# A fused attention and expert kernel on one core: VectorE's statistics, slots and residual moved within the group step, the rank matmuls one tile earlier

## The reference

```
h0  = layernorm(x)
g   = sigmoid(h0 @ Wg.T + bg)
h   = associative_scan of h[l] = (1 - g[l]) * h[l-1] + g[l] * h0[l], along the 1024 tokens
x1  = x + layernorm(h @ Wo.T + bo)
xf  = layernorm(x1)
eid = argmax(softmax(xf @ router_w + router_b))        # one of 8 experts
rank = running number of the token within its expert
y   = relu(xf @ w1[eid] + b1[eid]) @ w2[eid] + b2[eid] if rank < 320
      else relu(xf @ ow1 + ob1) @ ow2 + ob2             # overflow network, hidden size 1024
out = x1 + layernorm(y)
```

## Time and profile before

| | |
|---|---|
| median of 3 runs | 1272.75 us (1271.8 to 1273.87) |
| the profiled execution, its own time | 1271.02 us |
| its span, first to last instruction | 1269.3 us |
| granted TensorE clock, mean | 0.98 |
| PE busy | 1172.6 us, 92% of the span |
| DVE, POOL, ACT busy | 1003.3, 810.3 and 772.5 us |
| one step of the main loop, from one projection to the next | 552.84 to 586.09 us, 33.25 us |

### The profile page before, as it was taken

How to read it: one execution, slowest core, us unless ns; L and a number is a source line. 1 busy time by engine, 2 the same in 40 slices (tenths; PEclk the granted TensorE clock), 3 DMA queues, 4 the chain that set the end, 5 groups by cost and what they waited for, 6 DMA issues and landing times. The chain is left out here.

```text
span 1269.3 us, 24820 instructions
## 1 busy us (share of the span) xinstructions
PE 1172.6 (92%) x7705; PEld 1038.1 (82%) x7705; DVE 1003.3 (79%) x2731; ACT 772.5 (61%) x1362; POOL 810.3 (64%) x887
## 2 busy tenths in 40 slices
PE   4499999999999999999999999999999999889994
PEld 4388888888888888888888888888888888789994
DVE  4688888888888888888888888888888876578882
ACT  4265666666666666666666666666665655477773
POOL 4456666666666666666666666666666664436774
PEclk9699999999999999999999999999999999999997
DMA  7211111111111110100111110011111100334430
GB/s 242 83 35 50 51 47 44 38 37 34 33 33 33 33 33 33 33 26 24 33 33 33 33 33 25 25 33 33 33 33 33 33 17 18 104 112 168 149 103 31
DMA packets 59688, 65.32 MB, mean 51 GB/s; under 512 B 7836, under 2 KB 55886, under 8 KB 59525
## 3 DMA queue, kind: packets, MB, share of 16 engines
q1 hardware_dynamic: 52484, 59.58, 14.5%
q0 software_dynamic: 7168, 5.32, 1.4%
HBM read 40.17 MB, written 38.87 MB: 62 GB/s over the span
## 5 line engine op out<-in xcount | busy, mean ns | idle before, releaser
L362 POOL TENSOR_TENSOR rstd<-veps,mhalf 128x4 f32<-128x4 f32 (+1 forms) x144 | 179.4, 1246 | 355.1 <-DVE nmean L712 355.1
L539 ACT ACTIVATE hid<-psH,biasT 128x512 f32<-128x512 f32 (+1 forms) x320 | 209.1, 653 | 264.4 <-PE psH L1010 259.2
L1108 PE MATMUL psY<-W_hi,hid_hi 128*128 128x256 f32 x1216 | 351.2, 289 | 0.9 <-DVE hid_lo L833 0.9
L1111 PE MATMUL psY<-W_hi,hid_lo 128*128 128x256 f32 x1216 | 344.2, 283 | 0.0
L1110 PE MATMUL psY<-W_lo,hid_hi 128*128 128x256 f32 x1216 | 344.0, 283 | 0.0
L833 DVE TENSOR_TENSOR hid_lo<-hid,hid_hi 128x512 fp32r<-128x512 f32 (+1 forms) x320 | 266.0, 835 | 89.3 <-ACT hid_hi L543 83.8
L1008 PE MATMUL psH<-xfT_hi,W_hi 128*128 128x512 f32 (+1 forms) x640 | 246.1, 385 | 5.5 <-DVE xfT_lo L777 2.9
L1010 PE MATMUL psH<-xfT_hi,W_lo 128*128 128x512 f32 (+1 forms) x640 | 242.5, 379 | 0.0
L1009 PE MATMUL psH<-xfT_lo,W_hi 128*128 128x512 f32 (+1 forms) x640 | 242.3, 379 | 0.0
L1108 PEld LDWEIGHTS psY<-W_hi,hid_hi 128*128 128x128 f32 x1216 | 230.2, 189 | 10.5 <-DVE hid_lo L833 1.8
L1110 PEld LDWEIGHTS psY<-W_lo,hid_hi 128*128 128x128 f32 x1216 | 230.0, 189 | 6.7
(11 more groups left out here) (110 smaller groups left out, 2186.6 us busy)
## 6 DMA issues: line engine op xcount, KB each, us to landing
xin<-L_attn_x SPq DMA_DIRECT2D x32, 512.0 KB, 3.5
stage<-L_ffn_w SPq DMA_DIRECT2D x16, 1024.0 KB, 6.2
out<-outt SPq DMA_DIRECT2D x32, 512.0 KB, 2.9
xbuf<-zrow SPq DMA_DIRECT2D x1, 2570.0 KB, 18.5
xin<-xbuf SPq DMA_DIRECT2D x8, 257.0 KB, 5.5
stage<-L_ffn_ow SPq DMA_DIRECT2D x2, 1024.0 KB, 10.3
xbuf<-x,idx POOLq DMA_INDIRECT x128
b_b<-L_ffn_b SPq DMA_DIRECT2D x1, 1024.0 KB, 13.5
```

What stands on the lines that cost most here:

```text
L362: pool.tensor_tensor(rstd[k][:, 0:n], veps[k][:, 0:n], mhalf[:, 0:n], ALU.pow).then_inc(s_rs[k], 1)
L539: act.activation(hid[j % 2][:, 0:n], psH[:, j % 2, 0:n], ACT.Relu, bias=bias).then_inc(s_hid, 1)
L1108: pe.matmul(psY_t[:, t, :], hi, w[0][:, j, :], start=(j == 0 and t % 2 == 0), stop=False, skip_group_check=True)
L1111: last = pe.matmul(psY_t[:, t, :], lo_, w[0][:, j, :], start=False, stop=(j == HC - 1), skip_group_check=True)
```

## The change

Three queues are written in another order; no instruction is added or removed.

- **DVE.** `stats1(nxt)` comes directly behind `attended(nxt)`, ahead of `lo(2)`. `place(now)` comes behind `lo(2)`. Behind `lo(3)` stand `residual1(nxt)` and the four `bn_stats` of `stats2`, then `xn_lo(far)`, then the `moments` of `stats2`, and then `lo(4)` and `lo(5)`.
- **ACT.** `norm1(nxt)` comes ahead of `xn_hi(far)` and of tile 4's two activations, where it stood behind both.
- **PE.** `rank(now)` comes behind layer 1's tile 3 (the fourth), ahead of layer 2's tile 1, where it stood behind tile 4.

```diff
--- before.py
+++ after.py
@@ -618,11 +618,11 @@
                 if live(grp(i, u, -1), NG):
                     norm3(grp(i, u, -1), TG)
                 hidden(range(2, 4))
+                if up:
+                    norm1(nxt)
                 if ahead:
                     xn_hi(far)
                 hidden(range(4, 5))
-                if up:
-                    norm1(nxt)
                 if not ahead:
                     for j in range(4 * u, 4 * u + 4):
                         weights_hi((0, 0), j)
@@ -767,9 +767,13 @@
                 dve.wait_ge(s_u, cnt(g, 1, 1))
                 dve.tensor_tensor(x1[v][:, :, 0:D], att[:], xin[v][:], ALU.add).then_inc(s_x1, 1)
 
+            def read_rows2a(g):
+                dve.wait_ge(s_x1, cnt(g, 1, 1))
+                read_rows(2, lambda t: x1[g[1]][:, t, 0:D], TG)
+
             def stats2(g):
-                dve.wait_ge(s_x1, cnt(g, 1, 1))
-                stats(2, lambda t: x1[g[1]][:, t, 0:D], g, TG)
+                read_rows2a(g)
+                moments(2, g, TG)
 
             def xf_lo(g, n, base=0):
                 for c in range(DC):
@@ -879,19 +883,19 @@
                     choose(now)
                 if up:
                     attended(nxt)
+                    stats1(nxt)
                 low(2)
+                if run:
+                    place(now)
+                low(3)
                 if up:
-                    stats1(nxt)
-                low(3)
+                    residual1(nxt)
+                    read_rows2a(nxt)
                 if ahead:
                     xn_lo(far)
-                if run:
-                    place(now)
-                low(4)
                 if up:
-                    residual1(nxt)
-                    stats2(nxt)
-                low(5)
+                    moments(2, nxt, TG)
+                low(4, 5)
                 if ahead:
                     recurrence(far)
                 else:
@@ -1129,7 +1133,7 @@
                         layer1(now, j, GT, W1[1])
                         if j == 2 and live(grp(i, u, -1), NG):
                             pe.wait_ge(s_y, cnt(now, 2, 0))
-                        if j == 4:
+                        if j == 3:
                             rank(now)
                         layer2(now, j - 2, TG, W2[1])
                     if j == 3 and ahead:
```

## The result

| | before | after |
|---|---|---|
| median of the measurement | 1272.28 us (1271.61 to 1273.87, 4 runs) | 1282.64 us (1281.23 to 1284.62, 4 runs) |
| ratio, 95% interval | | 1.0081 (1.0063 to 1.0098) |
| span of the profiled execution | 1269.3 us | 1279.5 us |
| PE, DVE, ACT, POOL busy | 1172.6, 1003.3, 772.5, 810.3 us | 1169.3, 995.7, 766.5, 840.5 us |
| from one projection to the next, mean of 30 | 32.98 us | 33.48 us |

The change made the kernel slower by 10 us, and the forecast of 1255.5 us (1247 to 1268) was wrong. But this is not the kernel's only time: in the last group of experiments the same text took 1240.1 us against 1270.4, a ratio of 0.976.

A forecast was written before the change was run, and what follows sets the result against it. PE's queue, busy 92% of the span, was taken as the bound. Savings of 30 x 0.49 + 2.0 + 0.6 = 17.3 us from 1271.02 gave 1253.7, and 1.7 for the median gave 1255.5 us, range 1247 to 1268.

The forecast's parts named there:

- the chain: From `att`'s early statistics through POOL, `norm1`, residual and `tok2` to PE's transposes, forecast to start 0.49 us earlier each step.
- the gate's wait of 0.67 in all 30 steps: PE's `gate(far)` would wait for `xn_lo`, now behind the residual's reads, starting at 568.79 instead of 568.12.
- first rival: The gate hardly waits, POOL's `rstd` taking 1.0 instead of 1.4 or gate inputs coming closer: 1246.5 us, chance 0.10.
- Behind the loop: Last group's transposes gain 2.0 us of a 2.88 us wait, first expert's transposes 0.6 of 4.46.
- POOL is in `residual2` until 558.26 + 2.39 = 560.65: POOL's `rstd` for the early statistics could start only at 560.65, when `residual2` ends, instead of 559.61.
- third rival: `xn_lo`'s chain from POOL's `outt` makes the gate's wait outgrow the removed one: slower, 1276 us, chance 0.10.
- its point of 0.58 us on: Delay of the gate's chain, 0.49 + 2.6 / 30 = 0.58 us, from which the slower rival decides.
- Ranks and slots at nothing: Earlier rank matmuls on PE and `place` on DVE were both costed at nothing.
- the right cover: `place` takes the statistics' position ahead of `lo(3)`; were it gone, `lo(3)`, the residual and the gate would be late.
- these statistics run at their old length: On DVE, `att`'s statistics were taken to run beside POOL's `outt` at their old length.
- the sum: For `tok2`: two writes ahead of DVE's second scan, two behind `lo(6)`, ending at 576.94 instead of 577.68.
- the second rival: `tok2` is held off: three POOL writes stay behind `lo(6)`, each step saves 0.3 us: 1261 us, chance 0.18.

The follow-up runs named there:

- dispatch_first: Changed kernel with POOL's scatter DMAs (`dispatch`) ahead of norm 2 in its queue: 1238.74 us, and 1239.51 us in a second run.
- runs with one DMA: One scatter DMA per group instead of four, the other tiles' rows left out: 1242.94 us in the changed kernel, 1267.06 us in the kernel before.
- memset kernels: Changed kernel with memsets on POOL ahead of the scatter DMAs: three (0.8 us) took 1258.18 us, one (0.2 us) 1239.64 and 1240.23 us.
- norm 0 first: Changed kernel with norm 0 ahead of the third deviation on POOL: 1234.83 us with `dispatch_first`, 1300.21 us with the DMAs in the change's place.
- fourth group: Reruns on one chip: changed kernel unaltered 1283.02 us, kernel before 1270.77, `dispatch_first` 1239.51, norm 0 first without `dispatch_first` 1300.21.

## Why the prediction was wrong

**Where no release is late (1240.1 us), the chain was right in every other step.** Behind the projection I had `outt` until 7.81, the second `rstd` at 16.53, the gate at 15.95 with a new wait of 0.67, `tok2` from 18.51 to 24.10, the transposes at 24.40 without a wait. The step at 603.84 has 7.90, 16.57, 15.95 with 0.66, 18.50 to 24.14, and 24.46. The trade of one wait for the other is as described. That the gate agrees to 0.01 us is in part luck: I let `rstd` start directly behind `outt`, and it starts 0.18 us behind (it waits for `veps` and `nmean`, see the last section); against that, `nmr` took 0.20 us and not 0.30, and `norm1` follows it by 0.04 us, as it did in the earlier trace rows, where my sum has 0.12.

**The term that was mis-sized there is the gate's wait of 0.67 in all 30 steps.** In 13 it is nothing: `outt` starts 4.8 us behind the projection (576.94 - 572.16) instead of 5.5, and `rstd` and `nmr` of `deviation(3)` ahead of it take 1.04 and 0.20 us instead of 1.42 and 0.65, since no low half of DVE starts just ahead of either of them. My first rival had a `rstd` of 1.0 instead of 1.4, but the one in its sum is that of `deviation(1)`, which takes 1.39 us in both kinds of step; it had the result near (1246.5) and the place wrong. 13 x 0.66 is 8.6 us. The mean distance between projections fell by 32.98 - 32.06 = 0.92 us; of that the two waits explain 0.76 and 0.16 was not followed (5 us in all). Behind the loop 3.5 us are gained: the last `transposes1` waits 0.6 us instead of 3.0 (forecast 2.0), and the first expert's transposes 3.3 instead of 4.5 (forecast 0.6). The first projection comes 0.9 us later than in the kernel before, which the forecast doesn't have and no run explains. Together 30.2 us, the difference of the two spans; the medians differ by 30.3.

**Where releases are late (1282.64 us), the step that failed is "POOL is in `residual2` until 558.26 + 2.39 = 560.65".** It took over `outt`'s place from the kernel before, 5.42 us behind the projection, with its end at 7.81. It was 6.59, with the end at 8.99, by the late `ysb`. The gate's pause of 1.8 us instead of 0.67 outweighs the 1.16 removed: the mean distance is 33.48, 1.42 above the undisturbed 32.06, and 30 x 1.42 = 42.6 us is the difference between the two times (42.5). That is my third rival, "the gate's wait outgrows the one removed", from its point of 0.58 us on, with the place (POOL's `outt`) right and a cause that it didn't name. I gave it 0.10. The trace of before did show the late release, 0.04 and 0.65 us in turn at `ysb`; I never looked at that eviction, since PE's wait in the kernel before didn't hang on it.

**Ranks and slots at nothing is right in the sum, and says the wrong thing of what they do.** I named the right cover and the wrong reason for the gate to wait: with this part left undone the rest of the change costs about 51 us more (1291.4 against 1240.1, on two chips), since `psA` isn't free for the gate. No run shows what this part is worth where releases are late.

**The change needs these of its parts.** With no late releases: ScalarE's order and `xn_lo` undone 1286, rank and slots undone 1291, `xn_lo` ahead of the residual 1260 (with `dispatch_first`), all 1240. The place of `att`'s statistics was not undone by itself. The late releases fall on the whole change and hardly on the kernel before, whose wait at `tok2` hides 0.65 us.

**Still open** is what makes the increments late. What the runs show: where it occurred, it needed the scatter DMAs near layer 2's end (69 late with the changed kernel, 0 with the DMAs first, on the same occasion), and it needs something that differs between occasions with the same program. The runs with one DMA don't bear on this: on their occasion no run had a late increment, with four DMAs either. Whether that is the chip, its neighbours or where the program was loaded was not tried. All runs with late increments also lack more than half of the scatter DMAs' records, though `dispatch_first` lacks 812 with none late; and every timed run here was a recorded one (each has its span and clock), so the recording may itself have a part in it. The Trainium skill, page "NOTIFIC — the notification-queue block", section "7.1 Overflow: three behaviours, one of which stalls the engine", says that a full queue of records drops new ones, overwrites the oldest or stalls the producer, as it is set. The first two would fit the missing records and the third the late increments; one queue does not do both, and no run here shows any of them. The memset kernels and the one with ScalarE's old order were never run on an occasion with late releases.

The version to keep is `dispatch_first`: 1238.74 and 1239.51 us, one on either kind of occasion, against 1240 or 1283 for the change alone. With norm 0 first it took 1234.83 us, on one occasion.

## What to carry to other kernels

A change that removes a wait takes the slack from chains nobody looked at: before you forecast, follow the new critical chain back past the first engine that only "keeps its place", and look for waits there that are longer than the work they wait for. Run the unaltered kernel beside its variants before you credit an edit with a gain; four experiments agreed here with a theory that the plain kernel, on a further chip, corrected. And a buffer that serves three tenants (`psA`) makes the reader of the second one a waiter of the third.

## What was not expected of the hardware

- **A semaphore of PE can rise up to 1.8 us behind its matmul** while indirect DMAs of POOL are in flight (1.79 us in the step shown); on another occasion, with the DMAs at the same distance (4.04 us from the first issue to layer 2's end), not at all. In the page it looks like idle time with the releaser "remote" (60.3 us).
- **A small DVE instruction waits for a large one of POOL.** `veps`, 128 x 4 elements, took 1.41 us under `outt` and 0.17 us without it (DVE's rows above), and it ended 0.02 us behind `outt` (599.77 + 1.41, 598.76 + 2.40). The Trainium skill, page "SBUF — State Buffer", section "Who interferes with whom", says that `tensor_scalar` can enter a mode that takes the port pair shared with GpSimd, and that whoever is second is fully blocked. The trace agrees: in the first run of the changed kernel `veps` was held in 29 of 29 cases under `outt`, with a median of 1.9 us, and the median of the other 115 is 0.17 us. My prediction had told only half of that section (two SBUF inputs held, one free) and so let these statistics run at their old length. It cost little, since POOL's `rstd` stands behind `outt` anyway: it starts 0.18 us behind it.
- **The four `tok2` writes took 5.46 to 5.64 us** beside DVE's recurrence instead of 3.79, and it cost nothing, since they started 2.5 us earlier. In the step at 603.84 the four took 1.10, 1.95, 2.07 and 0.55 us: two were done within 0.2 us of the second scan's start and the third 0.34 us behind `lo(6)`, close to what the sum has. So the rule of that section held the writes, as the second rival said, but not for as long.
- **The granted clock fell to half behind some pauses of PE.** In the run of norm 0 first in the fourth group the gate's pause was 2.6 us in every other step and about 0.5 in the others, and these steps took 35.9 us instead of 32.3: 2.1 us by the longer pause, and some 1.5 by a granted clock of 0.50 for 3.4 us behind it. In the kernel before with `dispatch_first`, behind a pause of 2.2 us at the transposes (columns: stretch, its length, busy time of PE, PEld, DVE, ACT and POOL with counts, granted clock, DMA share, GB/s):

```profile
638.00:661.00 23.00, 23.00 (x153) 20.66 (x152) 19.69 (x52) 15.52 (x27) 16.68 (x19) 1.00 0.14 46
661.00:664.00 3.00, 0.96 (x9) 0.79 (x8) 1.73 (x5) 0.15 (x2) 2.16 (x4) 0.98 0.00 0
664.00:667.00 3.00, 3.00 (x16) 3.00 (x15) 2.28 (x7) 2.21 (x4) 1.20 (x1) 0.50 0.00 0
```

  The clock is 0.50 (1.2 instead of 2.4 GHz) for some 3 us once PE works again, and that step takes 35.4 us where its neighbour with the same pause takes 33.9. The 1.6 to 1.9 us of the changed kernel's gate cost no clock.
